# The down-projection of a transformer block by seven block products, with w1 and w2 in a ring of four blocks

## The reference

```
x = x + g_msa[:, None, :] * o                                     # o @ w_proj + b_proj
xn2 = _ln(x) * (1 + sc_mlp[:, None, :]) + sh_mlp[:, None, :]
h = jax.nn.gelu(xn2 @ w1 + b1, approximate=True)                  # w1: 576 x 2304
x = x + g_mlp[:, None, :] * (h @ w2 + b2)                         # w2: 2304 x 576
```

## Time and profile before

| | |
|---|---|
| median of 3 runs | 2652.15 us (2650.34 to 2652.68) |
| the profiled execution | 2651.53 us, span 2649.7 us |
| mean granted TensorE clock | 0.999 |
| PE busy | 2611.8 us (99%) |
| DVE, ACT busy | 1647.1 us (62%), 1467.4 us (55%) |
| time from one chunk's up to the next's | 122.3 us (1806.01 to 1928.35) |

### The profile page before, as it was taken

One profiled execution on the slowest core, in us unless ns is written; L12 is line 12 of the kernel. 1 busy time (PEld: TensorE's weight loads), 2 busy tenths in 40 slices (PEclk: granted clock), 3 DMA queues, 4 the chain that ended last, 5 costly groups with the idle time before them and its releaser, 6 DMA issues.

```text
span 2649.7 us, 42010 instructions
## 1 busy us (share of the span) xinstructions
PE 2611.8 (99%) x15820; PEld 1318.7 (50%) x15820; DVE 1647.1 (62%) x2677; ACT 1467.4 (55%) x2174; POOL 469.4 (18%) x339
## 2 busy tenths in 40 slices
PE   6999999999999999999999999999999999999999
PEld 3444444444444444444444334375757575666657
DVE  7788887788888788888888512344343535353421
ACT  4787787777777788788788786412121211111110
POOL 2532332222222222222222100110101010010100
PEclk9999999999999999999999999999999999999999
DMA  7513311133332123333333322402020211202000
GB/s 234 95 36 79 79 36 35 46 74 72 69 73 50 46 70 81 73 78 81 78 79 84 99 77 91 157 15 96 18 79 26 70 60 37 72 24 84 13 19 19
DMA packets 257862, 179.10 MB, mean 68 GB/s; under 512 B 172745, under 2 KB 211087, under 8 KB 256953
## 3 DMA queue, kind: packets, MB, share of 16 engines
q1 hardware_dynamic: 257370, 176.37, 25.0%
q10 hardware_dynamic: 288, 0.04, 0.0%
HBM read 96.49 MB, written 41.06 MB: 52 GB/s over the span
## 4 chain that ended last, share of the span: by engine, by line
PE 94%; DMA 1%; DVE 1%; SPq 1%; ACT 1%; issue 1%; POOL 0%; DVEq 0%; ACTq 0%
PE at_ps L1864 19%; PE at_ps L1200 18%; PE at_ps L1183 17%; PE at_ps L1890 14%; PE at_ps L1237 11%; PE at_ps L1211 8%; PE at_ps L1220 4%; PE at_ps L1883 1%; PE at_ps L1826 1%; PE at_ps L1843 1%; DMA ml_held<-head_rden 1%; PE at_ps L1261 1%; PE at_ps L1918 0%; DMA st_wm_first<-in_L_cond_b_mod 0%; SPq L486 0%
## 5 line engine op out<-in xcount | busy, mean ns | idle before, releaser
L755 ACT ACTIVATE at_p<-at_ps 128x1024 f32<-128x1024 f32 x1024 | 1040.0, 1029 | 330.9 <-PE at_ps L1183 326.3
L1200 PE MATMUL at_ps<-at_p,at_v 128*37 128x512 f32 x2304 | 590.3, 592 | 0.0
L935 DVE TENSOR_TENSOR at_rest_of_p<-at_p,at_pr 128x1024 bf16<-128x1024 f32 x448 | 553.0, 1234 | 15.4
L623 POOL TENSOR_TENSOR at_tssq<-at_tssq,power 128x8 f32<-128x8 f32 x112 | 276.7, 2470 | 880.6 <-DVE at_tssq L899 879.9
L1864 PE MATMUL at_ps<-ml_w2s,ml_hid 128*128 128x288 f16 x3348 | 414.9, 286 | 0.0
L1890 PE MATMUL at_ps<-ml_xhi,ml_w 128*128 128x512 f16 x1296 | 382.0, 379 | 0.0
L1864 PEld LDWEIGHTS at_ps<-ml_w2s,ml_hid 128*128 128x128 f16 x3348 | 327.5, 98 | 82.0
L1211 PE MATMUL at_ps<-at_pr,at_vr 128*101 128x512 f32 x896 | 365.1, 489 | 1.3 <-DVE at_pr L927 1.2
L927 DVE CAST at_pr<-at_p 128x1024 fp32r<-128x1024 f32 x448 | 314.6, 702 | 81.0 <-ACT at_p L755 78.9
L1183 PE MATMUL at_ps<-at_qk_even 109*64 109x512 f16 (+1 forms) x1536 | 308.7, 382 | 3.8 <-ACT at_p L755 2.6
L1183 PE MATMUL at_ps<-at_qk_odd 109*64 109x512 f16 (+1 forms) x1658 | 308.6, 381 | 0.3 <-ACT at_p L755 0.3
(11 more groups left out here) (189 smaller groups left out, 2365.3 us busy)
## 6 DMA issues: line engine op xcount, KB each, us to landing
head_sums<-at_oT SPq DMA_DIRECT2D x256, 72.0 KB
ml_held<-head_sums SPq DMA_DIRECT2D x64, 256.0 KB
at_xy<-in_L_cond_w SPq DMA_DIRECT2D x34, 288.0 KB
...
```

Of the source, the lines that this page charges most:

```text
L623: pool.tensor_tensor(tssq[:, 1, :], tssq[:, 1, :], keep.power[:, 0:QK], ALU.pow).then_inc(t_rstd, 1)
L755: act.activation(p[:, s % NP, :], ps[:, 2 * (s % 2):2 * (s % 2) + 2, :].rearrange("p a n -> p (a n)"), ACT.Exp).then_inc(exp_done, 1)
L935: nc.vector.tensor_tensor(rest_of_p[:, n % NL, :], p[:, s % NP, :], pr[:, n % NZ, :].bitcast(F32), ALU.subtract).then_inc(low_p_ready, 1)
L1200: last = nc.tensor.matmul(acc[a * HP:a * HP + RW, bank_of(U)], v32[:, (G % 2) * NT + 2 * s + a, h, :], p[:, s % NP, a * CH:(a + 1) * CH], ...
```

## The change

**Down-projection.** The 18 tiles f become 9 pairs (j, j + 9) (`PAIRS`). With the two halves of the hidden features, the two halves of a chunk's tokens and the two halves of the output columns, h @ w2 is a product of 2 × 2 blocks. One level of Strassen forms it from seven block products in place of eight. A block product is 9 pairs × 2 token tiles × 3 products of halves = 54 matmuls of 288 columns. In `tensor`, `down` runs them as idx 0 to 6 into three pairs of PSUM banks; ACT copies three of the results out (`take`), DVE folds the others onto them in `down` (L1939), multiplies by the gate and adds to x1 (`finish`).

**The left operands.** For each pair j, ACT runs two gelus; DVE makes five sums and differences of their four quarters (`mix`, 512 + 512 + 256 columns); ACT casts the seven operands (`high`: 512, 512 and 768 columns); DVE makes the seven low halves (512, 512 and 768 columns, `hidden`). The pieces for the next chunk's projection are placed by pair: `add_o`, `multiply_o` and ACT's `high_o` at the same j, `low_o` at a later one.

**The right operands.** Seven sums of w2's blocks are formed once, in the last attention group (`vector_blocks`, units 1 to 9), and stored as halves in HBM. The 18 slices of w2 leave the earlier groups; w1's 20 slices are regrouped.

**The ring.** w1 and w2 no longer stay in SBUF. Each chunk uses 12 blocks (5 of w1, 7 of w2, up to 1.33 MB each) that SP streams into a ring of four slots; block b is loaded once block b − 4 is used up.

```diff
+PAIRS = FT // 2
+RING, W1_BLOCKS = 4, 5
+BLOCKS = W1_BLOCKS + 7
-    SLICES = KC + 1 + KC * (MLP // H) + FT
+    SLICES = KC + 1 + KC * 4
-    MULTIPLY_AT, HIGH_AT, LOW_AT = ({f + at: k for k, f in enumerate((1, 4, 8, 11, 14))} for at in (0, 1, 2))
-    LATE = 4
-    WITH_DOWN = ((0, 1), (2, 3), (4,), ())
+    ADD_AT, LOW_AT = ({j: k for k, j in enumerate(at)} for at in ((0, 2, 4, 5, 7), (1, 3, 5, 6, 8)))
+    TURN_WITH = {2: (0, 1), 3: (2, 3), 4: (4,)}
...
+    def load_block(self, sp, J, b):
+        n = J * BLOCKS + b
+        slot = n % RING
+        if b >= RING:
+            self.block_used(sp, J, b - RING)
+        elif J:
+            self.block_used(sp, J - 1, b + BLOCKS - RING)
...
+        def high(J, j):
+            n = J * PAIRS + j
+            act.wait_ge(self.gelu_done, 2 * n + 2 + 2)
+            act.copy(self.hid[:, 5:7, j, 0, :], self.quarters(n)[:, 0:4:3, :]).then_inc(self.hhi_ready, 1)
+            act.wait_ge(self.mixed, 3 * n + 1)
+            act.copy(self.hid[:, 0:2, j, 0, :], self.mix[:, 0:2, :]).then_inc(self.hhi_ready, 1)
+            act.wait_ge(self.mixed, 3 * n + 3)
+            act.copy(self.hid[:, 2:5, j, 0, :], self.mix[:, 2:5, :]).then_inc(self.hhi_ready, 1)
...
         for J in range(self.CHUNKS):
             more = J + 1 < self.CHUNKS
-            for f in range(FT):
-                gelu(J, f)
-                if more and f in self.HIGH_AT:
-                    self.high_o(act, J + 1, self.HIGH_AT[f])
+            for j in range(PAIRS):
+                gelu(J, 2 * j)
+                gelu(J, 2 * j + 1)
+                high(J, j)
+                if more and j in self.ADD_AT:
+                    self.high_o(act, J + 1, self.ADD_AT[j])
...
-            for f in range(FT):
-                if J == 0 and f == FT - 1:
-                    dve.wait_ge(self.rden_stored, 16 * B)
-                hidden(J, f)
-                if J == 0 and f == FT // 2:
+            for j in range(PAIRS):
+                hidden(J, j)
+                if J == 0 and j == PAIRS // 2:
                     self.invert_den(dve, 1)
-                if more and f in self.MULTIPLY_AT:
-                    self.add_o(dve, J + 1, self.MULTIPLY_AT[f])
-                    self.multiply_o(dve, J + 1, self.MULTIPLY_AT[f])
-                if more and f in self.LOW_AT:
-                    self.low_o(dve, J + 1, self.LOW_AT[f])
+                if more and j in self.ADD_AT:
+                    self.add_o(dve, J + 1, self.ADD_AT[j])
+                    self.multiply_o(dve, J + 1, self.ADD_AT[j])
+                if more and j in self.LOW_AT:
+                    self.low_o(dve, J + 1, self.LOW_AT[j])
...
+        def down(J, turn):
+            for idx in range(7):
+                w = self.block(pe, J, W1_BLOCKS + idx).rearrange("p (j h n) -> p j h n", j=PAIRS, h=2)
...
+                if idx in (3, 4):
+                    pe.wait_ge(self.m_copied, 3 * J + idx - 2)
+                if idx >= 4:
+                    pe.wait_ge(self.down_step, 12 * J + (1, 3, 7)[idx - 4])
+                for j in range(PAIRS):
+                    if idx == 0:
+                        pe.wait_ge(self.hlo_ready, 3 * (J * PAIRS + j + 1))
+                    h = self.hid[:, A_OF[idx], j, :, :]
+                    for i in range(2):
+                        t = slice(i * P, (i + 1) * P)
+                        for n, (a, b) in enumerate(((0, 0), (0, 1), (1, 0))):
+                            last = nc.tensor.matmul(self.m_banks(idx)[:, i, :], h[:, a, t], w[:, j, b, :],
+                                                    start=(j == 0 and n == 0), stop=(j == PAIRS - 1 and n == 2))
+                last.then_inc(self.m_done, 1)
+                if turn and idx in self.TURN_WITH:
+                    self.turn_y(pe, J + 1, self.TURN_WITH[idx])
```

More of the change, by code:

```diff
@@ L531, in store_slice @@
             def store_slice(i):
-                src, half, r0, cols = slices[i]
-                n = src.shape[0]
-                for h, part in enumerate((word_hi, word_lo)):
-                    sp.dma_start(half[h, r0:r0 + n, cols].rearrange("p (a n) -> p a n", a=2), part[0:n]).then_inc(w_stored, 16)
+                src, _, places = slices[i]
+                for to, part in zip(places, word_of(i)[1:]):
+                    sp.dma_start(to, part[0:src.shape[0]]).then_inc(w_stored, 16)
             def unit(G, u):
@@ new lines, in block_used, with block, sync_blocks @@
+    def block_used(self, sp, J, b):
+        if b < W1_BLOCKS:
+            sp.wait_ge(self.up_ready, J * FT + min(4 * b + 4, FT))
+        else:
+            sp.wait_ge(self.m_done, J * 7 + b - W1_BLOCKS + 1)
+    def block(self, pe, J, b):
+        n = J * BLOCKS + b
+        pe.wait_ge(self.ring_loaded[n % RING], 16 * (n // RING + 1))
+        return self.ring[:, n % RING, :]
+    def sync_blocks(self, sp, u):
+        if 1 <= u <= PAIRS:
+            sp.wait_ge(self.w2_step, 4 * u)
+            for half, part in enumerate((self.w2_hi, self.w2_lo)):
+                sp.dma_start(self.halves.w2[:, :, u - 1, half, :].rearrange("m p n -> p m n"), part[:, :, :]).then_inc(self.w2_stored, 16)
+        if u < PAIRS:
+            if u == 0:
+                sp.wait_ge(self.ends.low_p_used, self.ends.all_splits)
+            if u >= 2:
+                sp.wait_ge(self.w2_step, 4 * u - 4)
+            for k in range(2):
+                f = u + k * PAIRS
+                sp.dma_start(self.w2_in[:, u % 2, 2 * k:2 * k + 2, :].rearrange("p a n -> p (a n)"), self.w2[f * P:(f + 1) * P, :]).then_inc(self.w2_in_loaded, 16)
@@ L1565, in sync_early @@
         if u == 8:
-            self.load_w1(sp)
+            for b in range(RING):
+                self.load_block(sp, 0, b)
         if u == UNITS - 1:
@@ L1663, in scalar @@
-            if more:
-                for k in range(KC):
+            for j in range(PAIRS):
[4 more added lines that the diff above has]
+                    self.high_o(act, J + 1, self.ADD_AT[j])
+            take(J, 0, self.part[:, 1, :].rearrange("p (i n) -> p i n", i=2), TPC * (J + 2) if more else TPC * (J + 1), 4 * J)
+            take(J, 1, self.corner[:, :, :], 0, 4 * J)
+            if more:
+                for k in self.TURN_WITH[2]:
+                    self.affine(act, J + 1, k)
@@ L1665, in scalar @@
+            take(J, 3, self.corner[:, :, :], 0, 4 * J + 1)
+            if more:
+                for k in self.TURN_WITH[3] + self.TURN_WITH[4]:
                     self.affine(act, J + 1, k)
@@ L1816, in vector @@
             if more:
-                project(J + 1, TPC + 2 * TPC * J)
-            down(J, (2 * TPC if more else TPC) + 2 * TPC * J, more)
+                project(J + 1, TPC + TPC * J)
+            down(J, more)
     def turn_y(self, pe, J, ks):
@@ L1882, in tails @@
                     side = slice((f % 2) * KT, (f % 2 + 1) * KT)
-                    last = nc.tensor.matmul(self.up_bank(f), self.w1[side, 8, cols(f)], self.xlo[side, KF, :], start=f in opening, stop=f in closing)
+                    last = nc.tensor.matmul(self.up_bank(f), w1(f)[side, 2 * KF, :], self.xlo[side, KF, :], start=f in opening, stop=f in closing)
                     if f in closing:
@@ L1909, in up @@
                 whole(n, False)
-        def last_tile(i, r, t):
-            pe.wait_ge(self.pair_taken, r - 1)
-            for half in range(2):
-                cols = slice(half * HALF, (half + 1) * HALF)
-                for f in range(FT):
-                    for n, (l, v) in enumerate(((self.hhi, 0), (self.hhi, 1), (self.hlo, 0))):
-                        last = nc.tensor.matmul(self.pair(i)[:, half, :], l[:, f, t], self.w2s[:, v, f, cols],
-                                                start=(f == 0 and n == 0), stop=(f == FT - 1 and n == 2))
-                last.then_inc(self.pair_ready, 1)
```

303 lines of the change are left out of this document (203 added, 100 removed).

## The result

The changed kernel takes 2727.2 us (2725.36 to 2728.49), 1.0286 times the kernel before (95% interval 1.0268 to 1.0303, before: 2651.24 us in the same rounds). The prediction said 2667. The profiled execution has a span of 2725.5 us.

The account below looks back on a forecast made before the run. PE's matmuls were taken as the bound. 2651.5 − 52.9 + 47.6 + 18.6 + 1.5 = 2666.3 us; with the 0.6 us by which the median stood above the profiled execution, about 2667 us, range 2645 to 2688.

Parts of the forecast that it names:

- What I cost at nothing: Waits within down, the transposes, the ring's loads and attention's `vector_blocks`: all forecast to add no time.
- my rivals: Clock holds 0.13; DVE and ACT lag less 0.09; `low_o` covered 0.03; no DVE overlap 0.12; ring or sums late 0.05.
- Term 1: Down: 54 fewer matmuls in each of 8 chunks at 0.1225 us, 52.9 us less.
- Term 2: Ahead of project: PE waits for the last `low_o` in seven chunks, +47.6 us, bounds +31.5 and +70.7.
- the walk: Up's DVE and ACT schedule, instruction by instruction: PE stands still 7.1 us before project, 9.2 in chunk 0.
- the two causes that the walk named: Up: ACT's lag from successive pairs with `add_o`, and the last `low_o` standing behind pair 8's gelus and `hidden`.
- The 4.2 us that I took off: Project, kernel before: PE's seven waits for the last `low_o`, subtracted from the forecast waits of 51.8 us.
- 963 assumed: DVE: a 768-column instruction taken as 0.963 us, midway between 512 and 1024 columns.
- Term 3: After the gap ahead of project: slow clock costs 2.65 us, seven times, +18.6 us, bounds 0 and 23.
- the choice between the rows: After PE's gaps: two rows with a slow stretch were followed, against chunk 0's row where the clock stayed 1.00.
- Term 4: End of the kernel: fold, gate product, addition and a larger store, 2.4 in place of 0.95 us, +1.5 us.
- The ring, `m_copied` and `down_step`: Down: PE was forecast not to wait for ring loads, ACT's copies or DVE's folds, at no cost.

Follow-up runs that it names:

- best2: Changed kernel with w2's loads ahead of stores, DVE's preparation at steps 5 to 7, b1's and ring's loads in unit 11, additions one pair earlier, `high_o` later: 2606.8 us.
- prep_left_out: Changed kernel without making w2's seven block sums; their place in HBM is filled with copies of w1's halves: 2664.7 us.
- prep_unit_later: Changed kernel with DVE taking each w2 pair, and SP storing it, one unit later, a semaphore for each load buffer: 2696.6 us.
- prep_behind: Changed kernel with DVE's three preparation parts moved from steps 0, 2 and 4 of a unit to 5, 6 and 7, behind `multiply_o`: 2702.8 us.
- load_first: Changed kernel with SP issuing a w2 pair's loads ahead of the store of the pair before, a semaphore per buffer: 2717.7 us.
- high_later: Changed kernel with ACT's `high_o` behind the next pair's two gelus instead of ahead of them: 2709.8 us.
- pieces_earlier: Changed kernel with `add_o` at pairs 0, 1, 3, 4, 6 and `low_o` one pair behind each: 2673.1 us.

## Why the prediction was wrong

**The step that failed** stands under "What I cost at nothing": "Attention loses 18 slices … and gets nine `vector_blocks` of about 6 us of DVE in the last group, where DVE was busy 23.91 of 100 us and PE was full: nothing either way." It cost 62.4 us. The share of busy time was right, and DVE's work cost nothing as work: best2 has all of it and starts up 6.4 us late. What I had not done is what I did for the MLP, walk through the instructions of one unit: the new wait for a load stands at step 0 on DVE; behind it stands `multiply_o`; behind that, on ACT, `high_o`, ahead of exponentials on which PE lives; and on SP the load stands behind a store that needs PE's last result. prep_left_out shows the size, prep_unit_later, prep_behind and load_first show three pieces of the loop, and best2 that opening them together gives 56 of the 62.4 us back with the same work and the same transfers. How the 62.4 us divide among the pieces is not shown; the edits don't add. None of my rivals had the loop, and so the range ended 39 us below the result.

**The other steps, measured.** Term 1, −52.9: a product takes 6.6 us, and best2's chunks are 6.6 us shorter; right. Term 2, +47.6: PE waited 49.5 us in seven waits, 9.3 in chunk 0 and 6.7 in each other, where the walk gave 9.2 and 7.1; right, with the two causes that the walk named (high_later takes one, pieces_earlier nearly all). The 4.2 us that I took off were misread: the earlier trace rows is the wait of the weight loads (PEld), and PE's own row, kernel before, 1650 to 2650, is shorter, so the term came to 49.5 − 2.3 = +47.2.

```profile
PE at_ps L1864 <- DVE ml_olo L1678: 2.3, 1, 2.3
```

The 768-column subtraction took 949 ns, 963 assumed. Term 3, +18.6: project took 15.27 to 16.45 us in place of 13.7, 1.6 to 2.7 us each, together +15.7; the choice between the rows was right, the size 0.4 us a gap too high. The granted clock was 0.50 behind the gaps looked at, of 5.1 (high_later), 6.7 and 9.3 us, and stayed at 1.00 behind one of 1.0 us (pieces_earlier), where all seven projects took 13.9 us. The Trainium skill, TensorE: Matmul & The Clock Gate, "What's actually happening", has the throttled state as the default, from which activity releases the array. The trace agrees with it: 0.50 after PE had stood still for 5.1 us and more, 1.00 again behind a stretch of work. Term 4, +1.5: from DVE's first instruction behind the last matmul to the end of the span 5.1 us in place of 3.2, +1.9. PE's waits for gelus in up are 1.4 us in place of 0.5, and one issue took 0.8: +1.7, which I did not have. This makes −52.9 + 47.2 + 15.7 + 1.9 + 1.7 = 13.6 for the 13.4 us. The ring, `m_copied` and `down_step` stopped PE nowhere, as predicted.

So the part that was walked through instruction by instruction came out to 1.4 us, with some luck in it (term 3 was 2.9 too high, and 1.7 that I had left out stood against it), and the part that was judged by its busy share was off by 62.
